# Softmax attention on one Trainium2 core: one DMA for the row of peaks, routing spread over the steps, the reciprocal one step later

## The chip, the cores and the metric

The program runs on one NeuronCore of a Trainium2 chip. The metric is the device time of one execution in microseconds (us), and less is better. The engines are named as in the profile: PE is the matmul engine (PEld its weight loads), DVE the vector engine, ACT the scalar engine, POOL the GpSimd engine, and SP the engine that here only issues DMAs.

## What is computed

Two layers, each a gated attention and a gated mixture of experts, on 64 sequences of 64 tokens with 256 channels. The change touches the first attention, a softmax attention over channels, and the routing of the first mixture of experts, which is computed beside it.

```python
def _L0_xattn_ref(x, c, Wq, bq, Wk, bk, Wv, bv, Wo, bo):   # 64 channels, 256 positions, 8 heads of 8
    q = split_heads(_proj(x, Wq, bq)); k = split_heads(_proj(c, Wk, bk)); v = split_heads(_proj(c, Wv, bv))
    q = _apply_rotary(q_emb, q)
    k = _apply_rotary(k_emb, k)
    scores = jnp.einsum('bhtc,bhsc->bhts', q, k) / math.sqrt(K_CH)
    p_attn = jax.nn.softmax(scores, axis=-1)
    out = jnp.einsum('bhts,bhsc->bhtc', p_attn, v)
    out = out.transpose(0, 1, 3, 2).reshape(b, N_HEADS * K_CH, t_t)
    return _proj(out, Wo, bo)

def _L0_ffn_ref(x, router_w, gate_proj, up_proj, down_proj):   # 8 experts, 2 for each token
    scores = jnp.einsum('btd,de->bte', x, router_w)
    routing_weights, routing_idx = jax.lax.top_k(jax.nn.softmax(scores, axis=-1), K)
    routing_weights = routing_weights / jnp.sum(routing_weights, axis=-1, keepdims=True)
    ...

x = x + jnp.tanh(g_xattn[0]) * _L0_xattn_ref(_layernorm(x), ctx_2048, ...)
x = x + jnp.tanh(g_ffn[0]) * _L0_ffn_ref(_layernorm(x), ...)
```

## The kernel before

The program is a row of stages; only the first, `stage_softmax_attention`, is touched. Its work is cut into 32 tiles of 128 rows (two sequences of 64), and the 16 "heads" of a tile are 8 heads for each of the two. Every engine runs its own loop over the same steps, `for i in every` with i from -5 to 34, in an order written by hand, and they meet at semaphores. A step i holds work on several tiles at once:

- PE multiplies queries by keys twice. The product A (`soft_pa`, for tiles i+1 and i+2) is made only to find the largest score of each row; the product B (`soft_pb`, tile i) is made again with one row more in `rep`, which holds the negated peak, so that PE subtracts it. `both(i, k)`, k from 0 to 7, does one eighth of each: two halves h, each B first and then A. Half h of A waits until DVE has read that half of the A before it (`a_done`).
- DVE takes the maxima of A: `maxima(i, k)`, two reductions (line 735). After the fourth (k = 3) the peaks of tile i+1 are whole, and PE turns them (line 877). ACT copies them out (line 664, `peak`), and SP writes them into `rep` of tile i+1 with four DMAs (line 543). PE waits for these before `both(i+1, 0)`.
- ACT takes the exponential of B (line 630); PE multiplies by the values (line 830, `values`); ACT copies the result out (`o_raw`, line 637, four groups); POOL issues eight DMAs (line 592) that pack numerators (`packed`) and denominators (`sums`) of tile i-1; DVE takes the reciprocal of the sums (line 782, at the end of step i); POOL multiplies (`on`, line 607); PE projects it a step later (line 894, between `both(i, 6)` and `both(i, 7)`, tile i-2).
- Ahead of all that PE projects queries and keys of tile i+4 (lines 846 and 847), DVE multiplies by cosines and sines (line 721), POOL adds them (`roped`, line 600) and splits them (`parts`, line 602), and SP spreads them into `rep` with twelve DMAs (line 504).
- The layernorm of tile i+5 needs statistics on DVE (lines 743 to 748), a root on POOL (line 582) and a product on DVE (`low`, line 762).

The routing of 16 of the tiles is a guest in these loops. `spread` (lines 149 to 156) takes the statistics of an output tile in steps 4 to 19; `choose` (lines 228 to 237) picks the two best experts, for four tiles at once, at the end of steps 9, 13, 17 and 21; `tally`, `rank`, `place`, `place_rows` and `weigh` turn picks into places and shares, at the ends of steps 21, 22, 23, 23 and 25 (RANK is 22). From step 24 POOL sends rows to their experts with four indirect DMAs in each step (line 364).

Of the kernel before, what the change touches and what calls it, by code (L numbers as in the profile page):

```python
# [12 lines left out]
fp32 = mybir.dt.float32  # L13
# [7 lines left out]
PART = 128  # L21
# [390 lines left out]
def stage_softmax_attention(nc, x_in, x_out, ctx, c):  # L412
# [11 lines left out]
    ROUTED, STRETCH, SENDS = MOE_TILES["moe0"][0], 4, 4  # L424
# [3 lines left out]
    with st:  # L428
# [77 lines left out]
        with nc.Block() as block:  # L506
            @block.sync
            def _(sp):
# [16 lines left out]
                for i in every:  # L525
                    if 0 <= i < len(blanks):
                        sp.dma_start(blanks[i].rearrange("(p r) d -> p (r d)", p=PART), blank[:]).then_inc(cleared[int(i >= CLEARS[0])], 16)
                    n = i + 3
                    if live(n):
                        sp.wait_ge(lo_ready, n + 1)  # L530
                        sp.wait_ge(hi_ready, n + 1)
                        sp.wait_ge(rep_init, min(n + 1, 4))
                        past(sp, b_ready, 2 * PAIRS * (n - 3))
                        fill_rows(sp, n, range(4 if n else 2))
                    if live(i - 3):
                        sp.wait_ge(xo_ready, i - 2)
                        sp.dma_start(x_out[i - 3], xo[:, (i - 3) % KEEP, :]).then_inc(stored[(i - 3) % KEEP], 16)
                    n = i + 1
                    if live(n):
                        sp.wait_ge(peak_ready, n + 1)  # L540
                        for j in range(4):
                            at = 32 * j + SPLIT
                            sp.dma_start(rep[at:at + 1, n % 4, :, 0:T].bitcast(fp32), peak[4 * j:4 * j + 4, n % 2, :].bitcast(fp32)
                                         ).then_inc(peak_in[n % 2], 16)
                    if (i + 9) % LOAD == 0 and 2 <= (i + 9) // LOAD < TILES // LOAD:
                        load((i + 9) // LOAD)
                    if i == 8:
                        held.load(sp)
                    if 0 <= i - 9 < held.RAWS:
                        held.load_raw(sp, c["L0_ffn_gate_proj"], c["L0_ffn_up_proj"], i - 9, i - 8)  # L550
# [10 lines left out]
            def _(pool):  # L561
# [8 lines left out]
                for i in every:  # L570
# [15 lines left out]
                    if live(t):  # L586
                        pool.wait_ge(o_out, GROUPS * (t + 1))
                        past(pool, on_ready, t - 1)
                        for j in range(4):
                            to = slice(32 * j, 32 * j + 32)  # L590
                            for row, dst in ((0, packed), (KC, sums)):
                                pool.dma_start(dst[to, t % 2, :], o_raw[32 * j + row:32 * j + row + KC, t % 2, :, :]
                                               ).then_inc(pack_in[t % 2], 16)
                    n = i + 4
# [9 lines left out]
                    if live(t):  # L604
                        pool.wait_ge(rsum_ready, t + 1)
                        past(pool, wo_ready, t - 1)
                        pool.tensor_tensor(on[:, t % 2, :], packed[:, t % 2, :], rsum[:], ALU.mult).then_inc(on_ready, 1)
# [7 lines left out]
            def _(act):  # L615
# [23 lines left out]
                for i in every:  # L639
# [22 lines left out]
                    if live(n):  # L662
                        past(act, peak_in[n % 2], 64 * (n // 2))
# [40 lines left out]
            def _(dve):  # L704
# [33 lines left out]
                for i in every:  # L738
# [10 lines left out]
                    if i == 4:  # L749
                        route.prepare(dve)  # L750
                    if routed(i - 4):
                        dve.wait_ge(xo_ready, i - 3)
                        route.spread(dve, i - 4, lambda t: xo[:, t % KEEP, :])
                    maxima(i, 1)
                    rope(i + 4, False)
                    maxima(i, 2)
                    maxima(i, 3)
                    rope(i + 4, True)
                    maxima(i, 4)
                    if live(new):  # L760
# [12 lines left out]
                    if i == RANK + 1:  # L773
                        route.place(dve)
                        route.place_rows(dve)
                    if i == RANK + 3:
                        route.weigh(dve)
                    t = i - 1
                    if live(t):
                        dve.wait_ge(pack_in[t % 2], PACK * (t // 2 + 1))  # L780
                        past(dve, on_ready, t)
                        dve.reciprocal(rsum[:], sums[:, t % 2, :]).then_inc(rsum_ready, 1)

            @block.tensor
            def _(pe):
# [5 lines left out]
                def both(i, k):  # L791
# [3 lines left out]
                    if live(i) and k == 0:  # L795
                        pe.wait_ge(peak_in[i % 2], 64 * (i // 2 + 1))
# [1841 lines left out]
```

## Time and profile before

| | us |
|---|---|
| median of three runs | 2602.62 |
| lowest and highest | 2599.2 and 2605.01 |
| profiled execution, its span | 2704.4 |
| in it, from the first B of tile 0 to the last of tile 31 | 58.87 to 641.65 |

The profiled execution is about 100 us longer than the timed ones. A "step i" below starts at the first matmul of B of tile i. "Granted clock" is the share of TensorE's full speed (2.4 GHz) that the chip granted; in a stretch it is 1.0 or 0.5, and a mean between tells how much of the time was spent at each. Ends of matmuls are modelled, so PE's busy time is not all work.

### The profile page before, as it was taken

The numbers are of one execution on the slowest core, as the hardware profiler recorded it, in microseconds if no ns is written. First come the engines' busy times: TensorE is split into PE (matmuls) and PEld (weight loads), VectorE is DVE, ScalarE is ACT, GpSimd is POOL, SyncE is SP. The second block draws the span as 40 slices with busy tenths as digits, with TensorE's granted clock in tenths as the row PEclk, the third lists the DMA queues.
The fourth block names the chain that finished last, engine by engine and source line by source line (L and its number), as shares of the span: only waits on it lengthen the run. The fifth ranks groups of instructions, "written<-read, shape, count | busy, mean of one in ns | idle before, by whom it ended". The sixth has DMA issues, their size and how long they took to land. (4 is left out here: it accounts for less than half of the span.)

```text
span 2704.4 us, 60407 instructions
## 1 busy us (share of the span) xinstructions
PE 2250.3 (83%) x20880; PEld 1699.7 (63%) x20880; DVE 1841.5 (68%) x3965; ACT 1152.8 (43%) x2509; POOL 1105.8 (41%) x1111
## 2 busy tenths in 40 slices
PE   6889989786878579994799899899888699998890
PEld 4555555443766357773677777787766577886670
DVE  4888888762547567775878878878876365444654
ACT  2777667554434223332344444444333354332230
POOL 2455555554144400001445445455577301325526
PEclk9898899765889689997999999999999799999995
DMA  5555455433358431211332332332334462445644
GB/s 115 125 134 141 121 137 131 113 114 100 104 178 277 133 130 52 64 31 51 82 83 62 81 85 59 81 87 57 85 100 135 134 206 90 142 148 167 200 153 144
DMA packets 249859, 313.10 MB, mean 116 GB/s; under 512 B 45152, under 2 KB 202848, under 8 KB 249056
## 3 DMA queue, kind: packets, MB, share of 16 engines
q1 hardware_dynamic: 188592, 219.11, 28.9%
q0 software_dynamic: 26624, 58.79, 7.9%
q10 hardware_dynamic: 34352, 31.34, 3.4%
q8 instruction: 180, 2.95, 0.5%
q14 instruction: 111, 0.91, 0.1%
HBM read 122.40 MB, written 102.24 MB: 83 GB/s over the span
## 5 line engine op out<-in xcount | busy, mean ns | idle before, releaser
L2119 POOL TENSOR_TENSOR ca_qk<-ca_qk,ca_q_swap 128x512 f32<-128x512 f32 x160 | 249.9, 1562 | 371.2 <-DVE ca_q_swap L2297 369.6
L735 DVE TENSOR_REDUCE soft_top<-soft_pa 128x2 fp32r<-128x512 f32 x512 | 328.4, 683 | 99.6 <-PE soft_pa L816 81.8
L630 ACT ACTIVATE soft_prob<-soft_pb 128x512 f32<-128x512 f32 x512 | 286.0, 594 | 191.8 <-PE soft_pb L809 171.9
L809 PE MATMUL soft_pb<-soft_rep 32*128 32x256 f32 x1024 | 213.4, 368 | 62.1 <-DVE soft_top L735 39.6
L809 PEld LDWEIGHTS soft_pb<-soft_rep 32*128 32x128 f32 x1024 | 140.1, 218 | 181.8 <-issue 85.8
L1440 PE MATMUL moe_pgu<-moe_w_hi,moe_xt_hi 128*128 x472 | 198.1, 420 | 39.8 <-DVE moe_xt_lo L1357 24.9
L816 PE MATMUL soft_pa<-soft_rep 31*128 31x256 f32 x1024 | 223.0, 375 | 6.0 <-DVE soft_top L735 3.5
L1459 PE MATMUL moe_py<-moe_w_d,moe_at 128*128 x788 | 219.1, 394 | 1.7 <-issue 0.8
L1363 DVE TENSOR_TENSOR moe_act_f<-moe_silu,moe_pgu 128x256 f32<-128x256 f32 (+1 forms) x236 | 88.5, 375 | 165.4 <-ACT moe_silu L1258 111.2
L2389 PE MATMUL ca_py<-ca_w_hi,ca_ot_hi 128*128 128x256 f32 x512 | 154.4, 302 | 33.1 <-DVE ca_ot_lo L2318 32.8
L1258 ACT ACTIVATE moe_silu<-moe_pgu 128x256 f32<-128x256 f32 (+1 forms) x236 | 82.1, 348 | 230.0 <-PE moe_pgu L1440 149.8
L1440 PE MATMUL moe_pgu<-moe_w_hi,moe_xt_lo 128*128 x472 | 175.1, 371 | 0.0
L1440 PE MATMUL moe_pgu<-moe_w_lo,moe_xt_hi 128*128 x472 | 174.9, 371 | 0.0
L2297 DVE TENSOR_TENSOR ca_q_swap<-ca_q_swap,ca_sin_q 128x512 f32<-128x512 f32 x128 | 115.7, 904 | 80.0 <-DMA ca_q_swap<-ca_q_f 75.3
L2181 ACT ACTIVATE ca_ot_hi<-ca_po 128x512 fp32r<-128x512 f32 x128 | 69.5, 596 | 235.8 <-PE ca_po L2487 218.6
L1179 POOL DMA_INDIRECT moe_yg<-moe_ys_rows,moe_held x112 | 114.8, 1025 | 130.9 <-DVE moe_xd L1327 41.6
L830 PE MATMUL soft_po<-soft_prob,soft_vaug 128*32 128x256 f32 x2048 | 168.0, 455 | 0.0
L2389 PE MATMUL ca_pp<-ca_ht_hi,ca_w_hi 128*128 128x512 f32 x312 | 139.1, 446 | 27.3 <-ACT ca_q_f L2167 21.1
L1357 DVE TENSOR_TENSOR moe_xt_lo<-moe_pt,moe_xt_hi 128x256 fp32r<-128x256 f32 x236 | 99.5, 422 | 81.0 <-ACT moe_xt_hi L1253 61.9
L1253 ACT ACTIVATE moe_xt_hi<-moe_pt 128x256 fp32r<-128x256 f32 x236 | 90.2, 382 | 149.1 <-PE moe_pt L1427 108.5
L816 PEld LDWEIGHTS soft_pa<-soft_rep 31*128 31x128 f32 x1024 | 143.4, 218 | 11.1 <-DVE soft_top L735 4.4
L364 POOL DMA_INDIRECT moe_rows<-moe_x_new,moe_held x80 | 78.1, 976 | 176.2 <-DVE moe_ys L1370 104.5
(377 smaller groups left out, 6384.7 us busy)
## 6 DMA issues: line engine op xcount, KB each, us to landing
ca_q_swap<-ca_q_f SPq DMA_DIRECT2D x640, 64.0 KB
moe_xs<-moe_rows SPq DMA_DIRECT2D x236, 128.0 KB
soft_rep<-soft_parts SPq DMA_DIRECT2D x378, 64.0 KB
moe_rows<-soft_blank SPq DMA_DIRECT2D x27, 768.0 KB
moe_ys_rows<-moe_ys ACTq DMA_DIRECT2D x134, 128.0 KB
moe_ys<-moe_ys ACTq DMA_DIRECT2D x102, 128.0 KB
moe_xd<-scratch SPq DMA_DIRECT2D x64, 128.0 KB
ca_vs<-ca_v SPq DMA_DIRECT2D x32, 256.0 KB
```

The costliest lines, as they stand in the source:

```text
L630: act.activation(prob[:, k % 4, h, :], p_b[:, 2 * T * h:2 * T * (h + 1)], ACT.Exp).then_inc(prob_ready, 1)
L735: dve.tensor_reduce(heads[:, j, :, g], p_a[:, 2 * T * h:2 * T * (h + 1)].rearrange("p (c s) -> p c s", c=HALF), AX, ALU.max).then_inc(a_do ...
L809: mm = pe.matmul(p_b[:, out], rep[of, i % 4, g, at:at + PART], rep[of, i % 4, g, 0:T], start=True, stop=True)
L816: mm = pe.matmul(p_a[:, out], rep[of, n % 4, g, at:at + PART], rep[of, n % 4, g, T:2 * T], start=True, stop=True)
L830: mm = pe.matmul(p_o[g % 2][32 * j:32 * j + 32, 0:T], vaug[:, i % 4, sc, 4 * g + j, :], prob[:, (2 * g + j // 2) % 4, j % 2, sc * T:(sc + ...
L1179: pool.indirect_dma_start(out=yg[:, t % HELD, k, :], out_offset=None, in_=ys_rows[h], in_offset=bass.IndirectOffsetOnAxis(ap=slot_id[:, t, ...
L1357: dve.tensor_tensor(xt_lo[:, b % 2, :, :], p_t[b % 2][:, 0:DIM].rearrange("p (k t) -> p k t", k=KC), xt_hi[:, b % 2, :, :].bitcast(fp32), ...
L1440: mm = pe.matmul(p_gu[b % 2][:, 0:W2], x[:, b % 2, k, :], w, start=(n == 0), stop=(n == 3 * KC - 1))
L1459: mm = pe.matmul(p_y[b % 2][:, 0:DIM], at[:, b % 2, m, :], w_d[:, bass.ds(e, 1), m, :].rearrange("p a d -> p (a d)"), start=(m == 0), stop ...
L2119: pool.tensor_tensor(qk[:, u % 2, m, :], qk[:, u % 2, m, :], q_swap[:, p % 2, :], ALU.add).then_inc(qk_ready, 1)
L2297: dve.tensor_tensor(out.rearrange("p (b s) -> p b s", s=SEQ), src.rearrange("p (b s) -> p b s", s=SEQ), tab[int(m == RQ)][:].unsqueeze(1). ...
L2389: mm = pe.matmul(out, x, y, start=start and n == 0, stop=stop and n == len(todo) - 1)
```

## The change

Five edits, all in the first stage. The row of peaks goes into `rep` with one DMA of 16 rows instead of four DMAs of 4. `choose` takes two tiles at a time, at the end of each odd step from 7 to 21. `place` moves from the end of step 23 to the middle of that step (`place_rows` stays), and `weigh` is cut into `share` at the end of step 24, `share_of` at the ends of 25 and 26, and `name_experts` at the end of 27. The statistics of the routed tile (`spread`) go behind `maxima(i, 1)`. And the reciprocal of tile i-2, instead of i-1, is taken in step i, between `maxima(i, 2)` and `maxima(i, 3)`, with POOL's product `on` behind the packing DMAs of tile i-1 and ahead of `roped`.

```diff
-    ROUTED, STRETCH, SENDS = MOE_TILES["moe0"][0], 4, 4
+    ROUTED, STRETCH, SENDS = MOE_TILES["moe0"][0], 2, 4
@@ sync
-                        for j in range(4):
-                            at = 32 * j + SPLIT
-                            sp.dma_start(rep[at:at + 1, n % 4, :, 0:T].bitcast(fp32), peak[4 * j:4 * j + 4, n % 2, :].bitcast(fp32)
-                                         ).then_inc(peak_in[n % 2], 16)
+                        sp.dma_start(rep[SPLIT:PART:32, n % 4, :, 0:T].bitcast(fp32), peak[0:HEADS, n % 2, :].bitcast(fp32)
+                                     ).then_inc(peak_in[n % 2], 16)
@@ gpsimd
+                    t = i - 2
+                    if live(t):
+                        pool.wait_ge(rsum_ready, t + 1)
+                        past(pool, wo_ready, t - 1)
+                        pool.tensor_tensor(on[:, t % 2, :], packed[:, t % 2, :], rsum[:], ALU.mult).then_inc(on_ready, 1)
                     n = i + 4
...
-                    if live(t):
-                        pool.wait_ge(rsum_ready, t + 1)
-                        past(pool, wo_ready, t - 1)
-                        pool.tensor_tensor(on[:, t % 2, :], packed[:, t % 2, :], rsum[:], ALU.mult).then_inc(on_ready, 1)
@@ vector
+                    maxima(i, 1)
                     if routed(i - 4):
                         dve.wait_ge(xo_ready, i - 3)
                         route.spread(dve, i - 4, lambda t: xo[:, t % KEEP, :])
-                    maxima(i, 1)
                     rope(i + 4, False)
                     maxima(i, 2)
+                    t = i - 2
+                    if live(t):
+                        dve.wait_ge(pack_in[t % 2], PACK * (t // 2 + 1))
+                        past(dve, on_ready, t)
+                        dve.reciprocal(rsum[:], sums[:, t % 2, :]).then_inc(rsum_ready, 1)
                     maxima(i, 3)
                     rope(i + 4, True)
                     maxima(i, 4)
+                    if i == RANK + 1:
+                        route.place(dve)
...
                     if i == RANK + 1:
-                        route.place(dve)
                         route.place_rows(dve)
-                    if i == RANK + 3:
-                        route.weigh(dve)
-                    t = i - 1
-                    if live(t):
-                        dve.wait_ge(pack_in[t % 2], PACK * (t // 2 + 1))
-                        past(dve, on_ready, t)
-                        dve.reciprocal(rsum[:], sums[:, t % 2, :]).then_inc(rsum_ready, 1)
+                    if i == RANK + 2:
+                        route.share(dve)
+                    if i - RANK - 3 in range(route.TOP):
+                        route.share_of(dve, i - RANK - 3)
+                    if i == RANK + 3 + route.TOP:
+                        route.name_experts(dve)
```

The waits of ACT and PE on `peak_in` count 16 instead of 64 for each tile.

On DVE, from the end of one step with routing through the middle of the next (`soft_pa` is A, `soft_top` the maxima), this stands before:

```order
L782 RECIPROCAL soft_rsum<-soft_sums 128x256
L735 TENSOR_REDUCE soft_top<-soft_pa 128x2 x2
L743 BN_STATS soft_stats<-soft_xt 128x6
L745 BN_AGGR soft_mv<-soft_stats 128x2
L748 TENSOR_SCALAR soft_var_eps<-soft_mv 128x1
L149 BN_STATS soft_r_stats<-soft_xo 128x6
L152 BN_AGGR soft_r_mv<-soft_r_stats 128x2
L156 TENSOR_SCALAR soft_r_var<-soft_r_mv 128x1
L735 TENSOR_REDUCE soft_top<-soft_pa 128x2 x2
L721 SCALAR_TENSOR_TENSOR soft_by_cos<-soft_px,soft_cols,soft_cos 128x256 x2
L735 TENSOR_REDUCE soft_top<-soft_pa 128x2 x4
L721 SCALAR_TENSOR_TENSOR soft_by_sin<-soft_px,soft_cols,soft_sin 128x256 x2
```

And this stands there after the change:

```order
L734 TENSOR_REDUCE soft_top<-soft_pa 128x2 x2
L742 BN_STATS soft_stats<-soft_xt 128x6
L744 BN_AGGR soft_mv<-soft_stats 128x2
L747 TENSOR_SCALAR soft_var_eps<-soft_mv 128x1
L734 TENSOR_REDUCE soft_top<-soft_pa 128x2 x2
L149 BN_STATS soft_r_stats<-soft_xo 128x6
L152 BN_AGGR soft_r_mv<-soft_r_stats 128x2
L156 TENSOR_SCALAR soft_r_var<-soft_r_mv 128x1
L720 SCALAR_TENSOR_TENSOR soft_by_cos<-soft_px,soft_cols,soft_cos 128x256 x2
L734 TENSOR_REDUCE soft_top<-soft_pa 128x2 x2
L760 RECIPROCAL soft_rsum<-soft_sums 128x256
L734 TENSOR_REDUCE soft_top<-soft_pa 128x2 x2
```

The reciprocal left the place ahead of the first maxima of a step and now stands ahead of the fourth, with which the peaks are whole.

On POOL, from the last packing DMA of a step to the start of the next, before:

```order
L592 DMA soft_sums<-soft_o_raw 32x1x256
L600 TENSOR_TENSOR soft_roped<-soft_by_cos,soft_by_sin 128x512
L602 TENSOR_TENSOR soft_parts<-soft_roped,soft_parts 128x2x256
L607 TENSOR_TENSOR soft_on<-soft_packed,soft_rsum 128x256
L576 TENSOR_TENSOR soft_xo<-soft_y,soft_xt 128x256
```

And after:

```order
L590 DMA soft_sums<-soft_o_raw 32x1x256
L596 TENSOR_TENSOR soft_on<-soft_packed,soft_rsum 128x256
L603 TENSOR_TENSOR soft_roped<-soft_by_cos,soft_by_sin 128x512
L605 TENSOR_TENSOR soft_parts<-soft_roped,soft_parts 128x2x256
L574 TENSOR_TENSOR soft_xo<-soft_y,soft_xt 128x256
```

The product `on` moved from behind `parts` to ahead of `roped`, and is of the tile before.

On SP, where the peaks are written (the difference of the two, in one of the first steps):

```order
 L504 DMA soft_rep<-soft_parts 8x8x256
-L543 DMA soft_rep<-soft_peak 1x4x256 x4
+L541 DMA soft_rep<-soft_peak 4x4x256
 L518 DMA soft_xt<-in_x 128x4x256
 L518 DMA soft_ct<-in_ctx 128x4x256
```

One DMA stands where four stood; nothing else on SP moves.

## Rows read from the trace of the kernel before

**Rows 1.** The page of the profile, its first line.

```profile
span 2704.4 us, 60407 instructions
```

**Rows 2.** Stretches: length, busy PE PEld DVE ACT POOL (count), granted clock, DMA share, GB/s.

```profile
58.87:641.65 582.78, 511.15 (x4609) 304.11 (x4610) 460.48 (x905) 387.08 (x831) 301.08 (x434) 0.85 0.49 126
177.53:228.36 50.83, 44.99 (x452) 27.79 (x452) 46.80 (x103) 38.47 (x84) 28.45 (x43) 1.00 0.56 135
322.48:371.92 49.44, 44.73 (x451) 27.71 (x451) 45.53 (x87) 38.25 (x85) 28.07 (x42) 1.00 0.57 161
228.36:247.44 19.08, 18.64 (x152) 10.94 (x152) 15.45 (x30) 11.94 (x27) 8.71 (x14) 0.73 0.51 112
247.44:266.12 18.68, 17.00 (x152) 10.04 (x152) 16.61 (x30) 13.24 (x30) 9.36 (x14) 0.86 0.51 140
301.38:322.48 21.10, 18.70 (x152) 10.94 (x152) 17.43 (x32) 12.39 (x29) 9.46 (x14) 0.76 0.36 108
371.92:394.21 22.29, 18.90 (x151) 11.15 (x151) 18.56 (x46) 12.68 (x29) 9.45 (x14) 0.77 0.40 90
441.17:464.25 23.08, 20.42 (x179) 13.49 (x179) 17.99 (x31) 12.14 (x26) 8.48 (x13) 0.85 0.46 117
522.93:545.10 22.17, 15.62 (x148) 9.13 (x144) 18.40 (x36) 12.59 (x27) 13.51 (x18) 0.85 0.44 114
```

**Rows 3.** Waits of PE from 58.87 to 641.65: us in total, times, longest.

```profile
PE soft_pb L809 <- DVE soft_top L735: 39.6, 42, 4.2
PE soft_pb L809 <- DMA soft_rep<-soft_peak: 12.6, 21, 2.0
PE soft_px L306 <- DVE soft_r_passed L282: 2.8, 1, 2.8
```

**Rows 4.** Timeline where step 15 starts: start, us, engine, line, what [idle before].

```profile
318.79 2.52 SPq L543 DMA_DIRECT2D soft_rep<-soft_peak  x4
...
322.48 0.38 PE L809 MATMUL soft_pb<-soft_rep 32*128 32x256 f32 x1 [0.25 <-DMA soft_rep<-soft_peak]
```

**Rows 5.** Timeline of DVE in step 15.

```profile
321.65 1.74 DVE L782 RECIPROCAL soft_rsum<-soft_sums 128x256 f32<-128x256 f32 x1
323.31 1.22 DVE L735 TENSOR_REDUCE soft_top<-soft_pa 128x2 fp32r<-128x512 f32 x2
...
329.67 1.29 DVE L735 TENSOR_REDUCE soft_top<-soft_pa 128x2 fp32r<-128x512 f32 x2 [0.49 <-PE soft_pa L816]
...
332.86 0.15 DVE L762 SCALAR_TENSOR_TENSOR soft_low<-soft_mv,soft_rstd 128x1 f32<-128x1 f32 x1
```

**Rows 6.** Timeline of PE in step 15.

```profile
329.10 0.38 PE L809 MATMUL soft_pb<-soft_rep 32*128 32x256 f32 x1
...
331.11 0.35 PE L809 MATMUL soft_pb<-soft_rep 32*128 32x256 f32 x1
...
334.96 0.70 PE L894 MATMUL soft_px<-soft_on,soft_w_out 128*128 128x256 f32 x2
```

**Rows 7.** Timeline of POOL in step 15, `roped`, directly behind the last packing DMA.

```profile
333.35 1.34 POOL L600 TENSOR_TENSOR soft_roped<-soft_by_cos,soft_by_sin 128x512 f32<-128x512 f32 x1
```

**Rows 8.** Timeline of DVE at `choose`, ends of steps 9 and 17.

```profile
226.31 0.36 DVE L228 MAX8 soft_r_top<-soft_r_score 128x8 f32<-128x8 f32 x4
...
227.67 1.74 DVE L782 RECIPROCAL soft_rsum<-soft_sums 128x256 f32<-128x256 f32 x1
...
372.44 1.27 DVE L231 TENSOR_TENSOR soft_r_weight<-soft_r_score,soft_r_top 128x32 f32<-128x32 f32 x1
```

**Rows 9.** Timeline of DVE at `weigh`, end of step 25.

```profile
522.61 0.28 DVE L327 TENSOR_TENSOR soft_r_weight<-soft_r_weight,soft_r_picked 128x128 f32<-128x128 f32 x1
...
528.27 1.21 DVE L735 TENSOR_REDUCE soft_top<-soft_pa 128x2 fp32r<-128x512 f32 x2
```

**Rows 10.** Timeline of ACT in step 25, behind POOL's sends.

```profile
510.20 1.08 ACT L630 ACTIVATE soft_prob<-soft_pb 128x512 f32<-128x512 f32 x2 [5.07 <-remote]
```

**Rows 11.** Timeline of POOL at the stage's end, packing of tile 31.

```profile
648.48 0.62 POOL L592 DMA_DIRECT2D soft_packed<-soft_o_raw  x1
```

More of the change, by code:

```diff
@@ L662, in _ @@
                     if live(n):
-                        past(act, peak_in[n % 2], 64 * (n // 2))
+                        past(act, peak_in[n % 2], 16 * (n // 2))
                         act.activation(peak[0:HEADS, n % 2, :], p_x[0][0:HEADS, T:2 * T], ACT.Copy).then_inc(peak_ready, 1)
@@ L795, in both @@
                     if live(i) and k == 0:
-                        pe.wait_ge(peak_in[i % 2], 64 * (i // 2 + 1))
+                        pe.wait_ge(peak_in[i % 2], 16 * (i // 2 + 1))
                     if live(n) and m == 0:
```

## The prediction

> **What bounds the kernel now.** I read the page first, for the span of the profiled execution [rows 1], then cut the touched stage into its steps, since the change is in nothing else. From the first B of tile 0 to the last of tile 31 it takes 582.78 us, with PE busy for 511 and DVE for 460 of it, at a mean granted clock of 0.85 [rows 2]. So PE bounds the stage, with DVE close behind, and part of PE's time is half speed. The reader is to see three kinds of step there. A plain step with routing takes 16.7 us at full clock (six steps in two stretches, 50.83 + 49.44 = 100.27, through 6), with PE busy for 15 and DVE for 15.4. Steps behind a `choose` of four tiles (10, 14, 18, 22) take 19.08, 21.10, 22.29 and 23.08. The step behind `weigh` (26) takes 22.17. In all of the last five the clock fell to 0.5 for a part of the step.
>
> Then the list of PE's waits [rows 3]: 39.6 us for DVE's maxima in 42 waits, 12.6 us for the DMA of the peaks in 21, and one of 2.8 us for `place`. The chain of waits of the whole program runs through later stages and says nothing here. These sums are the most that can be given back directly; half clock after a long wait comes on top.
>
> **Edit 1, one DMA of peaks.** Ahead of step 15 SP issues four DMAs from 318.79 for 2.52 us, and PE starts B at 322.48 after 0.25 us idle [rows 4]. Four issues in 2.52 us are 0.63 each, so one DMA instead of four is ready 1.9 us sooner, if its 16 rows land as fast as 4 do. PE's values matmuls fill that time to all but 0.25, so the wait goes whole and no more than that. Of the 12.6 us, 2.7 lie in the four `choose` steps, counted in edit 2; of the other 9.9 I take 8, as where PE next waits for ACT (`y`, ahead of line 846) starting sooner gains nothing. Bounds: 0 (the landing hides it) and 10.
>
> **Edit 2, choose by two.** Four tiles cost DVE 226.31 to 227.67, 1.36 us, and the reciprocal behind them another 1.66 to the next instruction (321.65 to 323.31) [rows 5, 8]. Steps 10, 14 and 18 exceed the plain 16.7 by 2.4, 4.4 and 5.6, in sum 12.4. Two tiles cost about 0.75, more with a collision. Where does it lie? In step 15 the last maxima end where the reciprocal starts, and A of the next tile is ready 0.57 after B starts (329.10 on PE, 329.67 on DVE [rows 5, 6]). So DVE has from 321.65 to 323.05 free, 1.4 us, once the reciprocal is gone. A `choose` of two fits; the eight of them are free, and 12.4 us go, with the half clock that the long stall set off. Step 22 has `tally` and `rank` too; at full clock I put it at 19.6, 3.5 less. Sum 15.9; bounds 9 (every piece collides, as the 1.27 us of one instruction in step 17 shows [rows 8]) and 18.
>
> **Edit 3, the reciprocal in the middle.** It leaves a place where DVE was idle anyway but for it, and goes where DVE is on PE's path. In step 15 the first maxima start at 323.31 and the fourth at 329.67, 6.36 us later with 0.49 idle [rows 5], so 5.87 of work; the fourth takes 1.29 more and ends at 330.96. PE's second half of `both(15, 4)` starts 0.15 behind, at 331.11 [rows 6]: it waits for just these maxima, and the turn of the peaks stands behind it. After the change DVE can start at 322.48 + 0.57 = 323.05, and the fourth maxima end at 323.05 + 5.87 + 1.66 + 1.29 = 331.87, 0.9 us later than now. Nothing behind it is idle long enough to take this back: from 331.11 to the next step PE is busy but for two waits of 0.25. So each step with maxima on this path grows by 0.9. Steps 2 to 23 have both; in four of them (10, 14, 18, 22) the delay of DVE's start goes too, and I count them in edit 2. That leaves 18 steps, 16 us lost. From step 24 on half clock makes PE slower than DVE, and nothing is lost. Bounds: 0 (PE at half clock, or A late, hides it) and 22 x 1.1 = 24.
>
> A wait of this size matters for the clock too. Step 11 has no `choose` ahead of it, yet spent part at half clock (mean 0.86) and took 18.68 against 16.7 [rows 2], 2 us; the clock fell there right behind one of the 42 waits for maxima of just under 1 us, while other waits of that length left it alone. With a stall of 0.6 to 0.9 in most steps I add three falls, 6 us; bounds 0 and 20.
>
> POOL's product `on` is now due in the step itself. `roped` starts at 333.35 directly behind the last packing DMA; `on` (0.7 us) in its place would end near 334.1, and PE's projection starts at 334.96, or 0.9 later still [rows 6, 7]. It has 0.9 to 1.8 us in hand, so it costs nothing in a plain step. If POOL is late by over 1.8 us, PE waits. `roped` comes 0.7 us later, and SP's twelve DMAs with it; they are needed three steps on.
>
> **Edits 4 and 5, place, weigh, spread.** `place` ahead of the fifth maxima takes away the 2.8 us wait but puts 2 us of DVE work on the path in the middle of step 23; with half clock avoided in step 24 I take 2 us gained. `weigh` and the reciprocal behind it hold DVE from 522.61 to 528.27 [rows 9], while A was ready 0.57 after 522.93, at 523.5: 4.8 us. Cut into pieces of 1 to 2 us it fits the 1.4 us gap. But in step 25 ACT stood 5.07 us, behind POOL's four sends, released by nothing that the profile names [rows 10]; it happens in 27 and 28 too, and step 26 will have it once `weigh` is not in its place. I take 2.5, bounds 0 and 5. `spread` behind `maxima(i, 1)` changes no sum.
>
> **The end.** Packing of tile 31 starts at 648.48 [rows 11], behind sends that waited for a reciprocal; with the reciprocal a step old it can start when ACT's last copy is done, 1.7 us sooner. 1.7 gained.
>
> **Sum.** -8 - 15.9 + 16 + 6 - 2 - 2.5 - 1.7 = -8.1 us, against a span of 2704.4. The median of the runs is 2602.62, 100 us under it; the profiled execution may have had more half clock. I carry the difference over as it is: **2594**.
>
> **A rule against this change.** One instruction of `choose` with two inputs in SBUF took 1.27 us where its like takes 0.16, as long as POOL's `parts` beside it [rows 8]. `low` (line 762) takes 0.15 at 332.86, 0.5 us ahead of POOL's `roped` at 333.35 [rows 5, 7]. After the change `low` comes 0.9 later, at 333.8, while `on` and `roped` fill POOL from 333.4 to 335.4. The Trainium skill (SBUF — State Buffer, Who interferes with whom) says that a VectorE instruction with two SBUF inputs and a GpSimd instruction that reads SBUF exclude each other for a whole instruction. By that rule the trace's 1.27 is no accident. As a mechanism of this kernel: `low` waits 0.3 to 1.6 us, the sixth maxima behind it have 0.77 us of slack, and PE loses up to 0.8.
>
> **Rivals.**
> - *The collision in every step.* 0.7 x 18 = 12.6 us more: 2607, no change within the measurement. For it speaks the order of times above; against it that the gaps move together with the step. 0.17.
> - *Slower: the stall in the middle lowers the clock.* If each step's 0.9 brings half clock in half of 20 steps, 10 x 2 = 20 instead of 6, and edit 3 costs 1.1 x 20 = 22 instead of 16, the sum is +12: 2614. It decides at about six falls more. 0.17.
> - *The middle hides it.* If PE reaches the fourth A later than in step 15, edit 3 costs 0.3 a step and no falls: 2602.6 - 8 - 15.9 + 5.4 - 6.2 = 2578. 0.18.
> - *POOL late.* If packing ends as late as in a few steps, PE waits 2 us for `on` in five steps, +10: 2604. 0.05.
> - My own sum, 2594 (2586 to 2602): 0.43.
>
> **How the numbers follow.** A measurement of this kernel tells about 0.2% (5.2 us) from no change. Faster by more, under 2597.4: three quarters of my own case (0.32) and the hidden middle, 0.50. Within it: the rest of my case (0.11), the collision (0.14 of 0.17), POOL late: 0.30. Slower: the clock case and the rest, 0.20. The range leaves out a part of the two outermost: 2574 to 2614.
>
> **What would show it.** Right: waits of PE for the DMA of the peaks near zero; no step from 9 to 22 over 20 us; DVE's fourth maxima start 0.9 later in the step than the 7.2 us of now, with a wait of PE of 0.6 to 0.9 for them; plain steps near 17 us. Wrong: plain steps at 16 us (middle hidden), `low` over 1 us in most steps (collision), mean clock of the stage under 0.85 (clock), waits of PE for `on`.

## The result

The changed kernel takes 2621.14 us (median of ten runs, 2616.16 to 2628.42) against 2605.51 for the kernel before on the same chip: a ratio of 1.0065 (95% interval 1.0043 to 1.0087), **slower** by 17 us by the ratio and by 16 between the two medians. The forecast was 2594, with a range of 2574 to 2614.

First a correction to the rows ahead of the prediction. The execution shown there [rows 1] spans 2704.4 us, 100 over its own runs. Of these 88 lie outside the stage (2704.4 - 582.78 = 2121.6, where the profiles below leave 2034), and its waits of 4 to 5 us that nothing named ends, beside POOL's sends [rows 10], come back in no later profile. So the kernel before was profiled once more (the run before_again below), and what follows is compared with that. Ahead of each row below stands the kernel it is from.

The changed kernel: first line of its page; stage B (first B of tile 0 to the end of tile 31) and steps 2 to 23 (length, busy PE PEld DVE ACT POOL, clock, DMA share, GB/s); PE's waits in the stage (total, times, longest); the group of `low`, the one-column instruction of line 768 (busy, mean ns).

```profile
span 2625.1 us, 60323 instructions
59.62:650.50 590.88, 522.43 (x4609) 307.27 (x4610) 473.66 (x917) 389.39 (x831) 303.47 (x437) 0.82 0.50 124
93.07:509.51 416.44, 365.53 (x3301) 217.12 (x3301) 352.79 (x699) 278.07 (x601) 202.05 (x302) 0.85 0.52 124
PE soft_pb L813 <- DVE soft_top L734: 32.5, 47, 2.5
PE soft_px L850 <- DVE soft_by_cos L720: 16.8, 25, 1.0
PE soft_px L850 <- ACT soft_y L699: 8.5, 12, 1.0
...
PE soft_pb L813 <- DMA soft_rep<-soft_peak: 0.7, 1, 0.7
L768 DVE SCALAR_TENSOR_TENSOR soft_low<-soft_mv,soft_rstd 128x1 f32<-128x1 f32 x27 | 30.6, 1134 | 0.0
```

The kernel before, once more (before_again): the same views.

```profile
span 2591.8 us, 60407 instructions
59.33:617.07 557.74, 493.57 (x4638) 295.93 (x4642) 457.95 (x905) 388.89 (x835) 303.23 (x437) 0.89 0.51 132
93.93:478.84 384.91, 346.32 (x3301) 210.49 (x3302) 337.56 (x701) 276.40 (x601) 202.75 (x302) 0.92 0.54 135
PE soft_pb L809 <- DVE soft_top L735: 29.3, 42, 3.5
PE soft_pb L809 <- DMA soft_rep<-soft_peak: 14.2, 21, 1.5
PE soft_px L846 <- ACT soft_y L700: 3.4, 10, 0.7
PE soft_px L846 <- DVE soft_by_cos L721: 3.2, 17, 0.2
L762 DVE SCALAR_TENSOR_TENSOR soft_low<-soft_mv,soft_rstd 128x1 f32<-128x1 f32 x27 | 13.9, 517 | 0.0
```

The spans differ by 33.3 us, and the stage by 33.1: the loss is all in it, and 31.5 of it in steps 2 to 23. (The runs say 17. The profiled execution of before_again was 12 us under the median of its kernel, and that of the changed kernel 6 over its own, so a difference between two profiles is a draw of the clock as well.) The wait for the DMA of the peaks is gone, 14.2 to 0.7, as meant. The new ones are small and many, and in steps 2 to 23 PE is *busy* for 19.2 us more with the same matmuls, at a mean clock of 0.85 instead of 0.92. The runs bear the clock out: over the whole program it was 0.910 on average in the ten of the changed kernel, and 0.918 to 0.921 in each set of runs of the kernel before. The row that tells most is the last: 27 instructions of one column took 1134 ns on average, where one alone takes 150 (the kernel before has a mean of 517).

Step 15 of the changed kernel starts at 333.64; DVE, then POOL, then PE (start, us, engine, line, what [idle before]).

```profile
336.62 1.29 DVE L734 TENSOR_REDUCE soft_top<-soft_pa 128x2 fp32r<-128x512 f32 x2 [0.38 <-PE soft_pa L820]
...
340.57 1.74 DVE L760 RECIPROCAL soft_rsum<-soft_sums 128x256 f32<-128x256 f32 x1
342.24 1.22 DVE L734 TENSOR_REDUCE soft_top<-soft_pa 128x2 fp32r<-128x512 f32 x2
...
345.35 1.25 DVE L768 SCALAR_TENSOR_TENSOR soft_low<-soft_mv,soft_rstd 128x1 f32<-128x1 f32 x1
346.52 2.66 DVE L734 TENSOR_REDUCE soft_top<-soft_pa 128x2 fp32r<-128x512 f32 x4
```

```profile
344.56 0.79 POOL L596 TENSOR_TENSOR soft_on<-soft_packed,soft_rsum 128x256 f32<-128x256 f32 x1
345.24 1.33 POOL L603 TENSOR_TENSOR soft_roped<-soft_by_cos,soft_by_sin 128x512 f32<-128x512 f32 x1
```

```profile
335.02 0.67 PE L850 MATMUL soft_px<-soft_xn,soft_w_in 128*128 128x256 f32 x2 [0.87 <-ACT soft_y L699]
339.52 0.70 PE L850 MATMUL soft_px<-soft_xn,soft_w_in 128*128 128x256 f32 x2 [0.96 <-DVE soft_by_cos L720]
343.01 0.35 PE L813 MATMUL soft_pb<-soft_rep 32*128 32x256 f32 x1 [0.71 <-DVE soft_top L734]
347.35 0.35 PE L813 MATMUL soft_pb<-soft_rep 32*128 32x256 f32 x1 [0.27 <-DVE soft_top L734]
```

`low` starts 11.71 into the step (345.35 - 333.64), where it started 10.38 into it before [rows 2, 5]. POOL's first product after the packing starts 10.92 into it, before 10.87 [rows 7]. So DVE moved by 1.33 us and POOL did not, and `low` now lies inside POOL's products. That is more than the 0.9 forecast; 0.38 of it is DVE idle for A ahead of the second maxima, where `spread` stood before. It ends at 346.60, 0.03 behind `roped` (345.24 + 1.33 = 346.57).

### The profile page after: what moved, and what is told of

Read it like the earlier page. It is cut to its first block and busy times, and to the rows that moved or that the text cites. A ratio compares the mean times of both kernels' runs of the same rounds, so it can differ in the third digit from the quotient of the medians.

```text
span 2625.1 us, 60323 instructions
## 1 busy us (share of the span) xinstructions
PE 2232.3 (85%) x20880; PEld 1682.2 (64%) x20880; DVE 1855.5 (71%) x3977; ACT 1156.5 (44%) x2509; POOL 1103.8 (42%) x1111
## 5 line engine op out<-in xcount | busy, mean ns | idle before, releaser
L1444 PE MATMUL moe_pgu<-moe_w_hi,moe_xt_hi 128*128 x472 | 192.2, 407 | 24.2 <-DVE moe_xt_lo L1361 13.9
L1463 PE MATMUL moe_py<-moe_w_d,moe_at 128*128 x788 | 211.6, 384 | 0.8 <-issue 0.8
L834 PE MATMUL soft_po<-soft_prob,soft_vaug 128*32 128x256 f32 x2048 | 177.4, 476 | 0.0
L2393 PE MATMUL ca_py<-ca_w_hi,ca_ot_lo 128*128 128x256 f32 x512 | 149.3, 292 | 0.0
L2393 PE MATMUL ca_py<-ca_w_lo,ca_ot_hi 128*128 128x256 f32 x512 | 149.0, 291 | 0.0
```

What stands on the lines that cost most here:

```text
L834: mm = pe.matmul(p_o[g % 2][32 * j:32 * j + 32, 0:T], vaug[:, i % 4, sc, 4 * g + j, :], prob[:, (2 * g + j // 2) % 4, j % 2, sc * T:(sc + ...
L1444: mm = pe.matmul(p_gu[b % 2][:, 0:W2], x[:, b % 2, k, :], w, start=(n == 0), stop=(n == 3 * KC - 1))
L1463: mm = pe.matmul(p_y[b % 2][:, 0:DIM], at[:, b % 2, m, :], w_d[:, bass.ds(e, 1), m, :].rearrange("p a d -> p (a d)"), start=(m == 0), stop ...
L2393: mm = pe.matmul(out, x, y, start=start and n == 0, stop=stop and n == len(todo) - 1)
```

## Experiments

**The theories.** T1: DVE's 1.66 us ahead of the fourth maxima are the loss. T2: `spread` behind the second maxima is. T3: `low` collides with POOL's `on` and `roped`. All ratios are against the kernel before on the same chip, with 95% intervals; 0.001 is 2.6 us. A `low` is called held where it takes over 0.25 us.

### One part of the change at a time

**before_again**: the kernel before, unedited.

> The kernel before, unchanged, profiled once more. The profile shown of it spans 2704.4 us, 100 over its own runs, so its steps can't be set beside those of other kernels. Outside of the stage the other kernels so far take 2034 to 2038 us. Expected: a span near 2602, a stage of 565 to 570 us, no waits of 4 us beside POOL's sends in steps 25, 27 and 28, and fewer falls of the clock in steps 2 to 24 than the kernel with the reciprocal in the middle.

It spans 2591.8, with a stage of 557.74, 7 us under the expected. Its clock was 0.92 in steps 2 to 23, and no ACT wait with no releaser stands beside the sends.

**b_recip**: the third edit alone.

```diff
+ (DVE, behind maxima(i, 2))   t = i - 2: reciprocal(rsum, sums[t])
- (DVE, end of the step)       t = i - 1: reciprocal(rsum, sums[t])
+ (POOL, ahead of roped)       t = i - 2: on[t] = packed[t] * rsum
- (POOL, behind parts)         t = i - 1: on[t] = packed[t] * rsum
```

> The kernel before with the third edit alone: the reciprocal of tile i - 2 between the third and the fourth maxima of step i, and POOL's product `on` ahead of `roped`. Theory 1 (the reciprocal on the path between DVE and PE is what the change loses by): 18 to 22 steps longer by 0.9, and falls of TensorE's clock behind the new waits of 0.7 in the middle of the steps, in sum 20 to 35 us slower. Theory 2 (`spread` behind the second maxima is the loss): this kernel costs only the 10 to 15 us of the sum less what a free end of the step gives in the steps behind a choice of four, so within 5 us of the kernel before. What I predicted for the edit: 16 + 6 = 22, less the share of edit 2 that needs no choice by two (about 7), so 15 us slower. Theory 3 (`low` collides with POOL's `on` and `roped`): `low` takes over 0.6 us in most steps.

1.0099 (1.0073 to 1.0125): 26 us slower, as much as the whole change or more (the intervals overlap). `low` took 37.8 us in 27, 23 of them over 0.8 us each. T1 and T3 both fit.

**b_spread**: `spread` behind `maxima(i, 1)` alone.

> The kernel before with `spread` moved behind the second maxima, and nothing else (16 routed steps, 4 to 19). My prediction gave this 0. Theory 2: the first rope product (`cos`) comes about 0.75 us later in each of 16 steps, PE waits 0.9 for it ahead of its second projection where it waited 0.2, and with falls of the clock this is 10 to 20 us slower. Theory 1: PE makes the wait good within the step, as DVE is ahead elsewhere: within 3 us of the kernel before.

1.0014 (0.9996 to 1.0032), at most 8 us, so T2 is not the loss. The wait for the first rope product is there, 13.2 us in 18 times, where it was 3.2:

```profile
PE soft_px L846 <- DVE soft_by_cos L721: 13.2, 18, 1.3
L762 DVE SCALAR_TENSOR_TENSOR soft_low<-soft_mv,soft_rstd 128x1 f32<-128x1 f32 x27 | 22.0, 815 | 0.0
```

The second row is a warning against counting held instructions: `low` is held here too, in nine steps for 1.60 to 1.66 us by `roped` alone, and yet the kernel loses at most 8 us. The first part of a hold costs PE nothing. PE waited 0.67 for the maxima behind a `low` of 1.65 (step 15 here), 0.88 behind one of 1.87 (step 16 of before_again) and 1.55 behind one of 2.54 (step 13 of b_on, below): 0.98 or 0.99 less each time, and so in step 15 of the changed kernel (1.25 held, 0.27 idle).

**b_choose**: `STRETCH` 2 instead of 4.

> The kernel before with the choice made for two tiles at a time instead of four, with the reciprocal still at the end of each step. By my sum the choice of two fits only where the reciprocal has gone, so that here each of eight steps loses 0.75 to 1.3 where four steps lost 2.4 to 5.6: 2 to 8 us faster, if the smaller stalls set the clock back in fewer steps. Rival: eight stalls of 1 us bring as many falls of the clock as four long ones, or more: 0 to 8 us slower.

0.9983 (0.9962 to 1.0004). Steps 10 to 21 and then step 22, first of the kernel before (before_again), then with the choice by two:

```profile
228.84:439.92 211.08, 190.46 (x1798) 115.52 (x1798) 185.12 (x385) 151.78 (x333) 112.10 (x167) 0.91 0.53 140
439.92:461.00 21.08, 19.95 (x178) 13.38 (x178) 16.31 (x28) 11.87 (x26) 7.88 (x13) 0.84 0.48 117
```

```profile
234.95:441.78 206.83, 187.94 (x1798) 113.49 (x1799) 182.45 (x394) 151.40 (x333) 112.13 (x167) 0.93 0.56 142
441.78:469.52 27.74, 25.14 (x179) 17.27 (x180) 18.04 (x28) 12.74 (x27) 8.87 (x14) 0.67 0.38 94
```

4.3 us are won in twelve steps, and step 22 loses 6.7 at a clock of 0.67. Step 22 took 21.08 to 23.08 in the two profiles of the kernel before and 27.74 here, so it may be this execution's; no run tells. The runs say 4 won in all, with an interval that reaches 1.

**b_peaks**: one DMA of the peaks alone.

> The kernel before with one DMA of the peaks instead of four, and nothing else. My prediction gave it -8 us (0 to -10): the wait of 0.25 for it goes, and larger ones where PE is early. What the runs so far suggest: PE's next wait, for ACT's `y`, grows from 0.25 to 0.67 by as much as the first one shrinks, and steps that start earlier bring `low` nowhere nearer POOL: 0 to 4 us faster.

0.9985 (0.9961 to 1.0009), about 4 us, with an interval that reaches 1. PE's waits in the stage, where the kernel before has 29.3, 3.4 and 14.2 in the rows above:

```profile
PE soft_pb L807 <- DVE soft_top L733: 33.5, 48, 4.2
PE soft_px L844 <- ACT soft_y L698: 8.4, 16, 0.9
PE soft_pb L807 <- DMA soft_rep<-soft_peak: 5.4, 7, 1.4
```

8.8 us of wait for the DMA went, and 5.0 came for `y` and 4.2 for the maxima: PE arrives earlier at the next engine and waits there.

**mix1**: the first, second and fourth edits, reciprocal and `spread` as before.

> The change without its third edit and without the move of `spread`: one DMA of the peaks, the choice by two, placement and shares in pieces, while the reciprocal stays at the end of the step. Theories 1 and 2 (these two edits are the loss): 10 to 20 us faster than the kernel before. Rival (the loss lies in the pieces on the boundaries, or the one DMA doesn't pay): no faster than the kernel before.

1.0000 (0.9981 to 1.0020). No loss, but not the 10 to 20 us of gain that I expected.

### Which half of the third edit

**b_on**: POOL's `on` a step later ahead of `roped`; DVE keeps the reciprocal at the end of the step.

> The kernel before, in which POOL's product `on` alone is taken a step later, ahead of `roped`, while DVE keeps the reciprocal at the end of the step. Theory 1 (DVE's 1.66 us ahead of the fourth maxima is the loss of the third edit): within 3 us of the kernel before. Rival (POOL's order is the loss: `on` late for PE's output projection, or `roped` and its rows late): 15 us or more slower.

1.0107 (1.0080 to 1.0135), 28 us slower, with DVE's order untouched. T1 is not needed for the loss. Its DVE and POOL in step 15:

```profile
345.42 1.56 DVE L763 SCALAR_TENSOR_TENSOR soft_low<-soft_mv,soft_rstd 128x1 f32<-128x1 f32 x1
```

```profile
344.94 0.80 POOL L598 TENSOR_TENSOR soft_on<-soft_packed,soft_rsum 128x256 f32<-128x256 f32 x1
345.62 1.33 POOL L605 TENSOR_TENSOR soft_roped<-soft_by_cos,soft_by_sin 128x512 f32<-128x512 f32 x1
```

345.42 + 1.56 = 346.98, again 0.03 behind the end of `roped`, though `low` had started inside `on`: the two products hold DVE up as one stretch of 2.0 us, where `roped` alone is 1.34. In ten of its 27 `low` took 2.53 or 2.54.

**a_short**: the changed kernel, the reciprocal over 16 of 256 columns from tile 1 on (the rest of `rsum` stays that of tile 0).

```diff
+ cut = T if t == 0 else 16
- dve.reciprocal(rsum[:], sums[:, t % 2, :])
+ dve.reciprocal(rsum[:, 0:cut], sums[:, t % 2, 0:cut])
```

> The changed kernel with the reciprocal at its place but over 16 of the 256 columns from tile 1 on (the other columns keep those of tile 0), so that DVE spends some 0.15 to 0.25 us in the middle of the step instead of 1.66. Theory 1: this takes away the cost of the place; with no reciprocal at the end of the step either, 20 us or more faster than the kernel before (2580 or less), 40 less than the changed kernel. Rival (POOL's order, or `spread`): still slower than 2605.

1.0013 (0.9984 to 1.0042). The reciprocals shrank from 54.0 us to 9.1. That is 14 us faster than the changed kernel, not 40, and no faster than the kernel before; my 2580 missed by 28. `low` took 41.1 us, the most of all:

```profile
L761 DVE RECIPROCAL soft_rsum<-soft_sums 128x16 f32<-128x16 f32 (+1 forms) x31 | 9.1, 292 | 21.3 <-DMA soft_sums<-soft_o_raw 21.3
L769 DVE SCALAR_TENSOR_TENSOR soft_low<-soft_mv,soft_rstd 128x1 f32<-128x1 f32 x27 | 41.1, 1521 | 0.0
```

DVE is earlier, so `low` comes sooner, still inside the stretch, and waits longer for its end. T1 falls as the main cause: 45 us of DVE's work away give back 14, and 10.5 of the 45 were spent again in `low`.

**a_low**: the changed kernel, `low` ahead of `maxima(i, 4)`.

> The changed kernel with `low` ahead of the fifth maxima instead of behind them, where POOL is still issuing the packing DMAs: 1.3 us earlier. Theory 3 (`low` collides with `on` and `roped` and this is a part of the loss): `low` takes 0.15 instead of 1.25 in most steps and the kernel gets 8 to 15 us faster than the changed kernel (2606 to 2613). Without theory 3: within 4 us of the changed kernel (2621).

1.0216 (1.0178 to 1.0254): 39 us slower than the changed kernel, where I had expected a gain. In step 15, DVE, POOL, PE:

```profile
379.82 2.43 DVE L765 SCALAR_TENSOR_TENSOR soft_low<-soft_mv,soft_rstd 128x1 f32<-128x1 f32 x1
```

```profile
380.21 0.79 POOL L596 TENSOR_TENSOR soft_on<-soft_packed,soft_rsum 128x256 f32<-128x256 f32 x1
380.90 1.31 POOL L603 TENSOR_TENSOR soft_roped<-soft_by_cos,soft_by_sin 128x512 f32<-128x512 f32 x1
```

```profile
382.99 0.55 PE L813 MATMUL soft_pb<-soft_rep 32*128 32x256 f32 x1 [2.36 <-DVE soft_top L734]
```

`low` started 0.39 *ahead* of `on` and was held all the same, until 0.03 behind `roped`. And the maxima that PE needs next stood behind it, so PE was idle for 2.36. The place was a few tenths of a microsecond too late: in this run `low` was held where it started up to 0.51 ahead of `on`, and ran free from 0.68 on. Where does the held stretch begin? Two steps of before_again stand on either side of the edge:

```profile
187.78 1.86 DVE L762 SCALAR_TENSOR_TENSOR soft_low<-soft_mv,soft_rstd 128x1 f32<-128x1 f32 x1
...
328.48 0.15 DVE L762 SCALAR_TENSOR_TENSOR soft_low<-soft_mv,soft_rstd 128x1 f32<-128x1 f32 x1
```

```profile
188.27 1.34 POOL L600 TENSOR_TENSOR soft_roped<-soft_by_cos,soft_by_sin 128x512 f32<-128x512 f32 x1
...
328.97 1.34 POOL L600 TENSOR_TENSOR soft_roped<-soft_by_cos,soft_by_sin 128x512 f32<-128x512 f32 x1
```

Both start 0.49 ahead of the recorded start of `roped`; one is held and one is free. In eleven of its 27 steps the kernel before ran within 0.01 of this edge.

### `low` where POOL only issues DMAs

```diff
+ (ahead of maxima(i, 3))   low = -mean * rstd
- (behind maxima(i, 4))     low = -mean * rstd
```

**a_low3**: the changed kernel with this edit.

> The changed kernel with `low` directly behind the reciprocal, ahead of the fourth maxima: by the profile of the changed kernel some 9 us into the step, while POOL issues the packing DMAs (7 to 11) and well over 1 us ahead of `on`. Theory 3, the only one that is left after the last runs (`low` can't run from about 0.5 us ahead of POOL's `on` or `roped` until `roped` ends, so each delay of 0.3 us or more in the step is turned into a stall of 1.2 to 2.5): all 27 `low` take 0.15, none of the 23 long ones is left, and this is 15 to 30 us faster than the changed kernel: 2590 to 2606. Theory 1 (DVE's 1.66 us ahead of the fourth maxima is by itself the loss): 2615 or more.

0.9962 (0.9938 to 0.9985): 2597.55 us, 27 us less than the changed kernel by the ratios (1.0065 - 0.9962 = 0.0103), from moving an instruction of 0.1 us. Steps 2 to 23; steps 7 to 14; the group of `low`; then DVE and POOL in step 15:

```profile
92.49:479.33 386.84, 329.68 (x3300) 197.91 (x3300) 330.69 (x702) 274.82 (x601) 201.74 (x301) 0.94 0.56 134
182.09:318.45 136.36, 112.70 (x1205) 68.03 (x1201) 120.94 (x268) 101.33 (x226) 75.19 (x112) 1.00 0.60 142
L763 DVE SCALAR_TENSOR_TENSOR soft_low<-soft_mv,soft_rstd 128x1 f32<-128x1 f32 x27 | 2.7, 99 | 0.0
```

```profile
326.83 0.09 DVE L763 SCALAR_TENSOR_TENSOR soft_low<-soft_mv,soft_rstd 128x1 f32<-128x1 f32 x1
```

```profile
329.16 0.80 POOL L596 TENSOR_TENSOR soft_on<-soft_packed,soft_rsum 128x256 f32<-128x256 f32 x1
```

Eight steps of 17.05 each at full clock. In step 15 PE still waits for the fourth maxima:

```profile
327.67 0.35 PE L813 MATMUL soft_pb<-soft_rep 32*128 32x256 f32 x1 [0.77 <-DVE soft_top L734]
```

Against the changed kernel steps 2 to 23 are 29.6 us shorter, and PE's busy time in them fell by 35.9 (365.53 to 329.68), while its idle time rose by 6. So the loss was not idle time: it is matmuls at half clock, which come with the held `low` and go with them. That one hold sets off one fall of the clock is not shown.

**b_recip_low3** and **b_on_low3**: b_recip and b_on with the same edit.

> The kernel before with the third edit alone and `low` ahead of the fourth maxima: the price of the place of the reciprocal without the collision. My sum had 0.9 in 18 steps (16), 6 for the clock, less some 7 for the free end of the step: 15 us slower than the kernel before if that term was right by itself. Theory 3 in its pure form (the place costs next to nothing, all of the 26 us is the collision): within 5 us of the kernel before or faster.

> The kernel before with POOL's `on` taken a step later ahead of `roped`, the reciprocal at the end of the step, and `low` ahead of the fourth maxima. Without the move of `low` this order was 28 us slower than the kernel before. Theory 3 (all of it was the longer stretch, `on` and `roped`, in which `low` can't run, and which begins 0.7 us earlier against it): within 5 us of the kernel before. Rival (the rows come 0.7 us later, or `on` is late for PE): 10 us or more slower.

1.0001 (0.9976 to 1.0027) instead of 1.0099, and 0.9996 (0.9971 to 1.0022) instead of 1.0107. T3 in its pure form: the third edit without the collision costs 0 against the kernel before, give or take 7 us, and so does POOL's order.

**b_low3** and **mix1_low3**: the kernel before, and mix1, with the edit.

> The kernel before with `low` ahead of the fourth maxima and nothing else. Its own profile has 7 to 9 collisions of 0.8 to 1.9 us in 27 steps. Theory 3: they go, with one or two falls of the clock: 8 to 15 us faster than the kernel before. Rival (these stalls fall where PE is behind anyway): within 4 us.

> The change without its third edit and without the move of `spread`, with `low` ahead of the fourth maxima. Theory 3: the first, second and fourth edit now give what their places take away, some 10 of the 18 to 26 that I had put on them, and the collisions of `low` another 8: 2580 to 2592. Rival: no faster than the kernel before with `low` moved alone.

0.9980 (0.9954 to 1.0005) and 0.9983 (0.9961 to 1.0006): 5 us each, less than forecast, and one and the same. b_low3 is also the control for the move itself: where few `low` were held, moving it gave 5, and where 16 to 24 were, 21 to 29. Beside b_low3 (same chip) the third edit costs 5 us, from -4 to 15 by the two intervals.

**a_low3_spread**: a_low3 with `spread` ahead of `maxima(i, 1)` again.

> The changed kernel with `low` ahead of the fourth maxima and `spread` back ahead of the second: the price of the move of `spread` without collisions. In the steps 7 to 16 of the kernel with `low` moved, 17.04 us each at full clock, PE waits 0.95 for the first rope product where it waited 0.19. If that wait is on the path: these steps come to 16.3 to 16.6 and the whole is 6 to 12 us faster than with `low` moved alone (0.996 becomes 0.992 to 0.994). Rival (`spread` early delays the second maxima, and PE waits there instead): the steps stay at 17.0 and the ratio at 0.996.

0.9990 (0.9970 to 1.0011), not faster. Steps 2 to 23, and then steps 14 and 15:

```profile
91.62:485.18 393.56, 351.54 (x3300) 210.80 (x3300) 329.47 (x704) 275.43 (x602) 203.26 (x302) 0.89 0.55 132
305.49:338.98 33.49, 29.32 (x300) 17.77 (x300) 29.78 (x67) 25.18 (x57) 18.82 (x28) 1.00 0.58 128
```

A plain step is 16.75 at full clock, 0.3 less than in a_low3. But the mean clock of steps 2 to 23 was 0.89, not 0.94. What is won in a step went back in clock in this execution; the runs can't tell the two kernels apart.

**best1** and **best2**: the kernel before with one DMA of the peaks, the choice by two and `low` ahead of the fourth maxima; best2 with the third edit too.

> The kernel before with one DMA of the peaks, the choice by two and `low` ahead of the fourth maxima; the reciprocal, `spread`, placement and shares where they were. Against the same with placement and shares in pieces (0.998): in that profile steps 24 to 27 took 75.3 us where the kernel before takes 68.0. If the pieces cost this, 0.994 to 0.996 here; if not, 0.998.

> As the one before, with the third edit as well (the reciprocal in the middle, `on` ahead of `roped`). By the steps so far the reciprocal in the middle costs 0.4 to 0.8 us in a plain step and gives back what a free end of the step is worth behind a choice: within 4 us of the one before, either way. If the third edit is worth its place once the collision is gone: 0.992 to 0.994.

0.9997 (0.9978 to 1.0017) and 0.9986 (0.9957 to 1.0016). The pieces of placement and shares are not to blame: in one execution each, steps 24 to 27 took 75.26 us in best1, with both in one piece, and 75.35 in mix1_low3.

**a_low3_again**: a_low3 once more.

> The changed kernel with `low` ahead of the fourth maxima, once more, on the chip's next occasion: its ratio to the kernel before was 0.9962 (0.9938 to 0.9985), the best of all so far. If that holds, 0.994 to 0.998 again, with all `low` at 0.1 us and steps 7 to 16 at 17.04 or less where the clock is full. If it was luck of the clock in that session, 0.998 to 1.001, as its relatives have.

0.9986 (0.9964 to 1.0008). Steps 2 to 23 once more:

```profile
91.80:481.45 389.65, 335.22 (x3304) 200.82 (x3300) 330.43 (x703) 275.47 (x602) 203.15 (x302) 0.93 0.55 133
```

Steps 6 and 7 are those of a_low3, 17.05 at full clock with the same waits; then steps 8 to 10 took 19.4 each at a mean clock of 0.80, with `low` at 0.1 throughout. Taken with the first, 0.9974, with an interval of about 0.9958 to 0.9990 if the two are independent: a_low3 beats the kernel before by some 7 us and the changed kernel by some 24. It is the best found, with a margin near what can be measured.

## Why the prediction was wrong

**The step that failed** is in the rivals: "the collision in every step", given 0.17 with the counterargument "that the gaps move together with the step". The mechanism was described rightly (a rule of the Trainium skill, SBUF — State Buffer, Who interferes with whom, pointed to it, and the traces agree: in all of them together 151 `low` took over 0.25 us, and 145 of these end 0.02 to 0.03 behind `roped`), and my own numbers had already decided it: `low` 0.9 later, at 333.8, and POOL busy from 333.4 to 335.4. Two engines' gaps move together only if the moved work stands ahead of both. POOL's packing waits for ACT's copies of the values, not for the fourth maxima; it stayed at 10.9 us into the step while `low` went from 10.38 to 11.71. Its chance should have been the largest.

**Its price** was mis-sized too: 12.6 us forecast, against 27 (a_low3 beside the changed kernel) and 21 by the repeat. I had counted PE's idle time, 0.7 in 18 steps. `low` did wait, in 23 of 27 steps (21 of them for POOL's products), for 30.6 us in all, but the rows of step 15 show 0.27 us of idle PE for it. What it cost is in the clock of steps 2 to 23: 0.85 against 0.94, and 0.93 in the repeat. How it gets there is open: the held `low` left PE idle for 0.27 in step 15 of the changed kernel and for 0.67 in that of b_spread, which lost at most 8 us in all.

**Edit 3, +16 +6.** The shape was right: with the collision away the plain steps are 17.05 (forecast "near 17"), and PE waits 0.77 for the fourth maxima (forecast 0.6 to 0.9). The sum was too large: b_recip_low3 costs 0 against the kernel before and 5 (-4 to 15) against b_low3, where 16 + 6 less 7 for the free end of the step makes 15. Nor do such waits by themselves bring the clock down: a_low3 has three of 0.67 to 0.95 in each of steps 7 to 16 and held full clock there, though its repeat, with the same waits in step 7, fell to half for parts of steps 8 to 10. So the slower rival, a stall in the middle that lowers the clock, had the right sign and the wrong cause: with the waits kept and the collision gone the loss was gone.

**Edit 1, -8.** About -4 (0.9985, from -10 to +2). I had written that starting sooner gains nothing "where PE next waits for ACT", and took off 1.9 for it; in the trace of b_peaks other waits took nearly all.

**Edit 2, -15.9.** About -4 (0.9983, from -10 to +1), in b_choose, where the reciprocal still stood in the place that the sum counted on. With that place free, edits 1 and 2 together are worth about the same: 1.0001 in b_recip_low3, 0.9986 in best2. I counted the excess of four steps as all due to `choose`, at rows with half clock in them; in before_again steps 10 and 14 have 19.1 and 19.2, not 19.1 and 21.1, and the clock falls elsewhere when it doesn't fall there. "No step from 9 to 22 over 20 us" held for 9 to 15, and failed for 16, 18 and 22 (20.38, 20.67, 24.92).

**Edit 4, -2 -2.5.** No gain and no cost that the runs show (best1 0.9997 without it, mix1_low3 0.9983 with it). The wait of 2.8 for `place` was real: it is in before_again too and gone in the changed kernel. ACT's wait of 5.07, by which 4.8 was cut to 2.5, was of one unusual execution.

**`spread` "changes no sum".** Wrong as to the wait: PE waits up to 0.96 for the first rope product in the 16 routed steps (3.2 us in the stage became 13.2 in b_spread, and 16.8 in the changed kernel), and DVE waits for A where `spread` had stood, which made `low` later still. By the time of the whole it was still right: 1.0014 by itself, and no difference with `low` moved.

**The sum itself.** -8.1 without the collision; a_low3, which is that kernel with `low` moved, measured -10 and -4. So the miss of the whole is the collision, which the sum put at nothing. The near match of the rest is partly luck, since edits 1 to 3 were each put too large and cancelled.

## What to carry to other kernels

When an edit delays one engine within a loop, list the instructions of the *other* engine that don't move with it, and lay both orders of time over each other again; a counterargument in words doesn't outweigh two start times that cross. An instruction whose mean is many times its shortest is the first thing to look for (here 1134 ns against 150), but what it costs is found by moving it, not by adding up how long it was held (22.0 us held in b_spread, at most 8 lost). Here it was cheaper to move it to a place where the other engine only issues DMAs than to shorten the work around it. And when small stalls lower the clock, their price stands in the busy time of the matmuls, not in the list of waits: a_low3 has more idle time of PE than the changed kernel and is 21 to 27 us faster.

## What the hardware showed

- A VectorE instruction of one column with two inputs in SBUF is held not for one GpSimd product but for a stretch of them back to back (`on` and `roped`, 2.0 us), to 0.02 or 0.03 us behind the last one's end, even where it starts inside the first.
- The stretch begins ahead of what the profile records: `low` was held for starts up to 0.51 us before the product's recorded start (a_low, step 11), and from 0.49 to 0.51 it was held in some steps and free in others. GpSimd was then still recorded as issuing the last packing DMA. Where it stood idle instead, waiting for DVE's `by_sin`, `low` ran in 0.15 though `roped` began 0.23 behind its start (before_again, 17.30 and 17.53). While it issued the earlier ones, `low` took 0.1 or 0.15 in the steps up to 24: that agrees with what the same section of the Trainium skill says of the generation of DMA descriptors (it infers that this needs the write side and not the reads). Six `low` in steps 25 and 26 of five kernels don't fit: they took 0.50 to 1.11 us with nothing but packing DMAs recorded on GpSimd (before_again, 526.37, 1.10), and what held them is open.
- Shortening DVE's reciprocals by 45 us in the stage (a_short) bought 14 us of time, and 10.5 of the 45 went into waiting for the end of the same stretch (`low` 41.1 us instead of 30.6).
- Why a_low3 kept full clock through ten steps with 2.4 us of waits in each, while a_low3_spread, with fewer, did not, and its own repeat did not in steps 8 to 10, stays open; no run was made for it.
